# Rows scattered into an expert-ordered table, the last batch routed in halves, shorter logits, and both ends of a two-layer kernel rewritten

## The reference, cut to what matters

```python
x1 = layernorm(x + window_attention(x))        # 16 heads, rotary, window of 64
x2 = layernorm(x1 + rwkv_channel_mix(x1))      # r, k, v products, relu squared
x3 = layernorm(x2 + linear_attention(x2))      # feature map, 16 heads
# last sublayer: a whole block with its own residuals, then the last layer norm
h  = layernorm(x3, ln1); x4 = x3 + causal_attention(h) @ Wproj
z  = layernorm(x4, ln2)                        # N = 4096 rows
gates = softmax(z @ Wgate); top 2 of 8 experts
pos = cumsum(mask, axis=0) * mask - 1          # place of a token among its expert's, in token order
keep = pos < capacity                          # capacity = 1024
exp_in[e, pos] = z[token]                      # (8, 1024, 256), zeros where nothing falls
exp_out = gelu(exp_in @ W1 + b1) @ W2 + b2     # 256 -> 1024 -> 256
x5 = x4; x5[token] += gate * exp_out[e, pos]
out = layernorm(x3 + x5)                       # the sum around the sublayer
```

## Time and profile before

| | |
|---|---|
| median of 3 runs | 1914.5 us (1913.64 to 1915.02) |
| the profiled execution: its time, its span | 1915.56 us, 1913.8 us |
| busy: TensorE, its weight loads | 1713.6 us (90%), 1106.0 us |
| busy: VectorE, ScalarE, GpSimd | 1018.5, 879.8, 831.4 us |
| mean granted TensorE clock | 0.948 |
| DMA | 124.17 MB, mean 65 GB/s |

### The profile page before, as it was taken

How to read it: one execution, slowest core, us unless ns; L and a number is a source line. 1 busy time by engine, 2 the same in 40 slices (tenths; PEclk the granted TensorE clock), 3 DMA queues, 4 the chain that set the end, 5 groups by cost and what they waited for, 6 DMA issues and landing times. The chain is left out here.

```text
span 1913.8 us, 32830 instructions
## 1 busy us (share of the span) xinstructions
PE 1713.6 (90%) x10804; PEld 1106.0 (58%) x10804; DVE 1018.5 (53%) x2375; ACT 879.8 (46%) x1855; POOL 831.4 (43%) x1247
## 2 busy tenths in 40 slices
PE   4798998999999999999989999998279999999970
PEld 3565765665477666556756545545246776666750
DVE  3457676868566986847698677775101110001115
ACT  2355463657755364765536566765031222222202
POOL 4574564522377552248663243324434333234220
PEclk9899999999999899999999999999589999999995
DMA  5615235032344222254502223420313332333115
GB/s 190 92 19 67 35 79 68 14 55 68 53 74 100 24 34 35 68 68 69 112 2 40 52 50 41 68 67 22 121 59 85 83 69 49 70 85 88 23 17 181
DMA packets 93059, 124.17 MB, mean 65 GB/s; under 512 B 14065, under 2 KB 63153, under 8 KB 92737
## 3 DMA queue, kind: packets, MB, share of 16 engines
q1 hardware_dynamic: 78560, 105.24, 26.8%
q0 software_dynamic: 14336, 16.83, 5.3%
HBM read 45.70 MB, written 25.56 MB: 37 GB/s over the span
## 5 line engine op out<-in xcount | busy, mean ns | idle before, releaser
L1026 ACT ACTIVATE b_probs<-b_psum 128x512 f32<-128x512 f32 (+3 forms) x896 | 417.9, 544 | 179.3 <-PE b_psum L896 177.7
L1277 DVE TENSOR_REDUCE b_mneg<-b_psum 128x2 f32<-128x384 f32 (+5 forms) x608 | 333.5, 593 | 94.0 <-PE b_psum L883 92.4
L1372 POOL TENSOR_SCALAR_AFFINE_SELECT b_probs<-b_probs 128x512 f32<-128x512 f32 (+1 forms) x400 | 240.0, 611 | 314.8 <-ACT b_probs L1026 304.3
L883 PE MATMUL b_psum<-b_qk 96*128 96x192 bf16 (+4 forms) x1280 | 298.9, 300 | 6.0 <-DVE b_before L1249 2.7
L896 PE MATMUL b_psum<-b_qk 99*128 99x192 bf16 (+5 forms) x1344 | 262.8, 290 | 9.7 <-DMA b_qk<-b_mrow 6.4
L1656 DVE TENSOR_TENSOR b_ye<-b_psum,b_b2b 128x512 f32<-128x512 f32 x32 | 22.1, 692 | 428.9 <-PE b_psum L1611 428.9
L1635 ACT ACTIVATE b_hid<-b_psum,b_b 128x512 f32<-128x512 f32 x128 | 88.0, 687 | 317.9 <-PE b_psum L1602 317.9
L1564 POOL DMA_INDIRECT before_last_norm<-b_ye,b_ids x64 | 99.5, 1555 | 301.0 <-DMA before_last_norm<-b_ye,b_ids 156.2
L1611 PE MATMUL b_psum<-b_w,b_hid 128*128 128x256 f32 x1024 | 222.4, 379 | 0.8 <-ACT b_hid L1635 0.8
L1602 PE MATMUL b_psum<-b_xgt,b_w 128*128 128x512 f32 x512 | 221.7, 594 | 0.0
L1611 PEld LDWEIGHTS b_psum<-b_w,b_hid 128*128 128x128 f32 x1024 | 193.9, 190 | 27.6 <-ACT b_hid L1635 1.6
(11 more groups left out here) (212 smaller groups left out, 2431.6 us busy)
## 6 DMA issues: line engine op xcount, KB each, us to landing
b_qk<-b_split SPq DMA_DIRECT2D x372, 128.0 KB, 4.9
b_w<-in_W SPq DMA_DIRECT2D x16, 1024.0 KB, 7.8
b_src<-in_x SPq DMA_DIRECT2D x4, 1024.0 KB, 6.2
before_last_norm<-b_early SPq DMA_DIRECT2D x4, 1024.0 KB, 4.9
b_o<-before_last_norm SPq DMA_DIRECT2D x4, 1024.0 KB, 5.4
before_last_norm<-b_o SPq DMA_DIRECT2D x4, 1024.0 KB, 4.5
normed<-b_y SPq DMA_DIRECT2D x4, 1024.0 KB, 5.2
b_rows<-before_last_norm SPq DMA_DIRECT2D x8, 512.0 KB, 7.8
```

The costliest lines, as they stand in the source:

```text
L883: ins = pe.matmul(out[:, i, :], q[0:KS, h, P * t:P * t + P], q[0:KS, HG + h, a:e], start=not last, stop=True, skip_group_check=True)
L1026: act.activation(probs_of((g, h2, t), a, e)[:, heads[0]:heads[-1] + 1, :], bank, ACT.Exp, scale=SCALE).then_inc(s.exp_done, 1)
L1277: dve.tensor_reduce(out, in_bank(("max",) + x[1:], heads, e - a), AX.X, ALU.max, negate=True).then_inc(s.max_read, 1)
L1372: ins = pool.affine_select(out=block, in_=block, pattern=[[0, HG], [1 if ahead else -1, z - y]], compare_op=ALU.is_ge, fill=none, base=y - ...
```

## The change

- **Straight into an expert-ordered table.** `normed` and its store `z_out` are gone. A table `slot_rows` in DRAM has one row for each of the 8 x 1024 slots. SP fills it with zeros early (`zeros`, 8 DMAs of 1 MB). When a batch's slot numbers are known (`spot`, the first half of the old `place`), GpSimd scatters the z rows from `y` there, 128 rows of 1 KB per DMA, 16 DMAs per batch (`put`), beside the 16 entry scatters. `y` is free when the puts have landed. In the experts' block SP loads each expert's rows with two plain DMAs (`load_tokens`); the gathers are gone, and the entries are needed only for gates and for the way back, so they are turned in the middle of the first expert.
- **Halves.** The last batch's routing from `logits` on is done in two parts of four tiles. The first part's puts are issued before the block ends, the second part's and all entry scatters after.
- **Logits.** Four products side by side, in four groups of 32 columns: the gate weights (padded to 32 columns) are the stationary operand, half of the part's tokens move through each. ScalarE copies the result back, and one small product per tile (`choose`) with a matrix of two ones per column adds the two halves of the contraction and turns it.
- **Start.** The identity and x come first, in halves; the first projection's weights have a semaphore of their own; small constants are issued by ScalarE and waited for at the first use in layer 0.
- **End.** The last expert's hidden parts are ordered by columns (512, 256, 256) with the values of finished columns between them, and its last two tiles are passed on singly. The last norm stands in the experts' block, without a block's end before it; its table is loaded behind the last Gelu. GpSimd computes scale and shift, ScalarE applies three rows of four and VectorE one.

```diff
+        self.AHEAD = {("place", B - 1): 25.0, ("put", B - 1): 25.0}
-                  [self.known(*x, self.batch[g] - 1) for x in (("z_out",), ("z_turn", 1, 1), ("x4", 3))]))
+                  [self.known(*x, self.batch[g] - 1) for x in (("put", TOPK - 1, NT - 1), ("z_turn", 1, 1), ("x4", 3))]))
+        for e in range(E_):
+            add(("zeros", e), "SP", 0.5, ("rotate", 0, 7), ("divide", e // 4, e // 2 % 2))
...
+        parts = self.parts_of(b)
+        for r, tiles in enumerate(parts):
+            size = len(tiles) / NT
+            before = ("place", r - 1, b) if r else self.known("place", 0, b - 1)
+            add(("logits", r, b), "PE", 0.25 + 0.87 * size, ("z_take", tiles[-1] // 4, 1, b))
+            add(("logit_take", r, b), "ACT", 0.1 + 0.42 * size, ("logits", r, b))
+            add(("choose", r, b), "PE", 1.6 * size, ("logit_take", r, b))
...
+            add(("spot", r, b), "DVE", 1.1 + 0.4 * size, ("position", r, b), ("index", r, b),
+                *[self.known(kind, TOPK - 1, NT - 1, b - 1) for kind in ("put", "scatter") if not r])
+            add(("place", r, b), "DVE", 0.9 + 0.4 * size, ("spot", r, b), ("gates", r, b))
+            if b < B - 1 or r + 1 < len(parts):
+                for kind, ready in (("put", "spot"), ("scatter", "place"))[:1 if self.halved(b) else 2]:
+                    for k in range(TOPK):
+                        for t in tiles:
+                            add((kind, k, t, b), "POOL", 1.28, (ready, r, b))
...
+def put_rows(pool, u, k, t, z_slots, rows_put):
+    pool.indirect_dma_start(
+        out=z_slots, out_offset=bass.IndirectOffsetOnAxis(ap=u.write_at[:, k, t:t + 1], axis=0),
+        in_=u.y[:, t, :], in_offset=None, bounds_check=E_ * CAP - 1, oob_is_err=False).then_inc(rows_put, 16)
...
+                        for side in range(2):
                             for c in range(NC):
+                                k = NC * side + c
+                                ins = pe.matmul(out[32 * k:32 * k + 32, 0:n], u.wgate[:, c, :],
+                                                u.xtr[:, c, P * tiles[0] + n * side:P * tiles[0] + n * side + n],
+                                                start=True, stop=True, tile_position=(0, 32 * k), skip_group_check=True)
+                    elif kind == "choose":
...
+                            ins = pe.matmul(out[:, E_ * t:E_ * t + E_], u.xtr[:, 0, at:at + P], u.pairs[:, i // n, :],
+                                            start=True, stop=True)
...
+                        if b and not x[1]:
+                            dve.wait_ge(slots_gathered, 16 * TOPK * NT * b)
+                            dve.wait_ge(rows_put, 16 * TOPK * NT * b)
+                        ins = dve.tensor_tensor(u.write_at[:, :, some], place, keep, ALU.add)
...
                     if not windowed[g] and not plan.place_of(g) and b:
-                        dve.wait_ge(s.z_out, 16 * b)
+                        dve.wait_ge(rows_put, 16 * TOPK * NT * b)
...
@@ experts, SP
+            sp.wait_ge(rows_put, 16 * TOPK * NT * B)
+            load_tokens(sp, 0, u, s, z_slots)
+            load_tokens(sp, 1, u, s, z_slots)
+            load_expert(sp, 1, u, s, w1_dram, w2_dram)
             sp.wait_ge(slots_gathered, 16 * TOPK * NT * B)
             sp.dma_start(u.slot_rows[:, :, :], slots_dram.rearrange("(r p) o -> r p o", p=P)).then_inc(s.rows_in, 16)
...
+            sp.wait_ge(s.summed, 16 * E_ * CT)
+            for h in range(HALVES):
+                sp.dma_start(u.rows[:, 4 * h:4 * h + 4, :], rows(x4_dram, h)).then_inc(rows_in[h], 16)
@@ experts, GpSimd
+            for k in range(TOPK):
+                for t in LAST_TILES:
+                    put_rows(pool, u, k, t, z_slots, rows_put)
+            for k in range(TOPK):
+                for t in range(NT):
+                    scatter_entry(pool, u, k, t, slots_dram, slots_gathered)
...
+                link(pool.tensor_tensor(scales, root, root, ALU.mult))
+                link(pool.tensor_tensor(scales, scales, u.last_var[:, four], ALU.mult))
+                link(pool.tensor_scalar(scales, scales, -0.5, 1.5, ALU.mult, ALU.add))
+                link(pool.tensor_tensor(scales, scales, root, ALU.mult))
+                link(pool.tensor_tensor(u.shifts[:, four], u.last_mv[:, four, 0], scales, ALU.mult))
+                pool.tensor_scalar(u.shifts[:, four], u.shifts[:, four], -1.0, None, ALU.mult).then_inc(last.scale_ready, 1)
...
@@ experts, TensorE, last expert
+                for part, whole in enumerate((pieces_of(e)[:2], pieces_of(e)[2:3], pieces_of(e)[3:])):
+                    ahead = min(NF * (part + 1) + 2, len(parts))
+                    for k, x in parts[begun:ahead]:
+                        hidden(e, k, *x)
+                    begun = ahead
+                    pe.wait_ge(s.h_done, 16 * e + NF * (part + 1))
+                    for tiles in whole:
+                        values(e, tiles)
...
@@ set-up, ScalarE
+            act.wait_ge(cleared, 1)
+            act.dma_start(u.wgate[:, :, 0:E_], a["wgate"]).then_inc(later, 16)
+            for n in LATER_SMALL:
+                act.dma_start(made[n][:], a[n]).then_inc(later, 16)
+            for n in LATER_ROWS:
+                act.dma_start(made[n][:, :], a[n].partition_broadcast(P).rearrange("p o d -> p (o d)")).then_inc(later, 16)
             take_turned(act, u.xa[:, :, 1:T + 1], u, s, 0)
+            act.dma_start(slots_dram.rearrange("(r p) o -> r (p o)", p=P), a["empty"]).then_inc(later, 16)
+            act.dma_start(x4_dram[N:N + P, :], a["spare_rows"]).then_inc(later, 16)
```

More of the change, by code:

```diff
@@ L56 @@
 EARLY = 1
+HALVED = True
 BANK = 512
@@ L216 @@
                 "back": "keep",
-                "oc_turn": "oc_take", "oc_pj": "oc_y", "z_turn": "z_take", "logits": "top", "position": "place",
+                "oc_turn": "oc_take", "oc_pj": "oc_y", "z_turn": "z_take", "logits": "logit_take", "choose": "top", "position": "spot",
                 "o_turn": "o_take", "pj": "y1", "x1_turn": "x1_take", "r": "r_low", "k0": "relu", "v0": "gated",
@@ L447, in describe_norm, with parts_of, part_with, halved @@
                     self.add((out + "_dve", t + 2, b), "DVE", 0.35, (name + "_scale", h, b), read[1])
+    def parts_of(self, b):
+        return [range(NT)] if not self.halved(b) else [range(4), range(4, NT)]
+    def part_with(self, b, t):
+        return [t in tiles for tiles in self.parts_of(b)].index(True)
+    def halved(self, b):
+        return HALVED and b == B - 1
     def describe_route(self, b):
         add = self.add
-        add(("x3_in", b), "SP", 3.0, ("x3_out", b), self.known("out1", 3, b + 1), self.known("x4_out", b - 1),
-            self.known("z_out", b - 1))
+        add(("x3_in", b), "SP", 3.0, ("x3_out", b), self.known("out1", 3, b + 1), self.known("x4_out", b - 1))
         for h in range(2):
@@ L841, in _ @@
                     b = plan.batch[2 * g]
+                    if t == 0 and not g:
+                        pe.wait_ge(first_weights, 32)
                     if t == 0 and not first:
@@ L1097, in _ @@
                             dve.wait_ge(s.src_in, 16 * b)
+                        if not b and not x[1]:
+                            dve.wait_ge(later, LATER_COUNT)
+                            dve.tensor_scalar(u.bk[:, :], u.bk[:, :], 1.0, None, ALU.add)
+                            chained(dve.tensor_scalar(u.bq_plus[:, :], u.bq[:, :], 1.0, None, ALU.add))
                         ins = sum_and_stats(b, x, "pj", u.src, u.src, u.norms[0])
@@ L1198, in _ @@
                     elif kind == "top":
-                        done(dve, b, "logits")
-                        chained(dve.tensor_copy(u.lg[:, :, :].rearrange("p t e -> p (t e)"), bank_of("logits", b)[:, 0:NT * E_]))
-                        for t in range(NT):
+                        some, n = part_of(b, x[1]), len(plan.parts_of(b)[x[1]])
+                        done(dve, b, "choose", x[1])
+                        chained(dve.tensor_copy(u.lg[:, some, :], routed_bank("choose", x[1], b)[:, some, :]))
@@ L1719, in statistics @@
+            link = dve_chain(dve, last.dve_chain)
+            def apply(h):
+                dve.wait_ge(last.scale_ready, h + 1)
+                i = 4 * h + 3
+                dve.tensor_scalar(u.rows[:, i, :], u.rows[:, i, :], u.last_mv[:, i, 0:1], u.scales[:, i:i + 1],
+                                  ALU.subtract, ALU.mult).then_inc(last.dve_ready, 1)
+            for h in range(HALVES):
                 dve.wait_ge(rows_in[h], 16)
@@ L1866, in _ @@
             dve.memset(u.ones16[:, :], 1.0)
-            dve.wait_ge(loaded, 16 * (count + 3))
+            dve.memset(u.wgate[:, :, :], 0.0).then_inc(cleared, 1)
+            dve.wait_ge(rows_in[0], 32)
+            for i in range(2):
+                dve.tensor_tensor(u.pairs[:, i, :], u.id32[:, 64 * i:64 * i + E_], u.id32[:, 64 * i + 32:64 * i + 32 + E_], ALU.add)
+            dve.wait_ge(loaded, 16 * count)
             for i, t in enumerate(bf16_tables):
```

485 lines of the change are left out of this document (245 added, 240 removed).

## The result

The kernel after takes 1867.04 us (median of 4 runs, 1865.49 to 1870.92) against 1914.07 (1913.3 to 1915.02) in the same comparison: ratio 0.9753, 95% interval 0.9739 to 0.9768. The forecast was 1871.0 with 0.95 on faster. The profiled execution is the fastest of its four (1865.49 us, span 1863.7, clock 0.959); the spans differ by 50.1, the medians by 47.0.

What follows compares the result with a forecast made beforehand. TensorE bounds attention and experts; about 170 us around them are serial. Terms -10.5 + 4 - 19.9 + 0.5 - 13.3 - 4.3 = -43.5 take 1915.56 to 1872.1, 1871.0 for the median; range 1857 to 1888.

Steps and rivals of the forecast that it cites:

- Set-up: Before the first projection: reordered loads, with ScalarE issuing 13 DMAs at 0.48 us, start it at 14.4; gain 10.5 us.
- Attention: Attention stage: logits gain 3 us, puts cost 6, zero fills 1; sum +4 us (-3 to +20).
- the 6 charged: Attention stage: cost of GpSimd's added puts, 2 us for each of three batches (0 to 15).
- until the second half's z is turned nothing changes: Last batch: its path stays as before up to that turn, at 1342.4 us; no cost put there.
- The 1.6 us per put: GpSimd's puts: price if VectorE's two-port operations keep it from writing descriptors; time some 5 us later.
- The hold of `y`: Attention, batch 3: y comes free near 1297 us, and waiting outputs cover the 32 us; 0 charged, 5 at the other end.
- The rival of a re-planned order: Attention stage: queues planned anew with truer scatter costs cut TensorE's idle time by 8 us, to 1863; chance 0.10.
- Last batch: From the last z to the experts: half routing and direct puts start TensorE at 1378.5 instead of 1398.35; gain 19.9 us.
- Behind the last product: After the last expert: earlier scatter-adds and no block's end (3.3) before the norm; gain 13.3 us (10 to 14).
- The stall that I say is included: Last expert: 1 us of extra TensorE stall, said to be included in the 13.3 us gain.
- Last norm: Final norm: work shared with GpSimd and ScalarE gives a period of 2.45 us per half batch; gain 4.3 us (0 to 6).
- The lock that the earlier trace let one fear: Last norm: VectorE and GpSimd exclude each other on SBUF; 0.2 or so a half, 2 us in all.

Runs made afterwards that it cites:

- e10: Kernel after with the attention block closed without GpSimd's drain, repeated with more rounds; 1863.05 us, ratio 0.9731 to the kernel before.
- e2: Kernel after with the last batch routed whole instead of in halves, drain kept; 1870.99 us, ratio 0.9777 to the kernel before.
- e3: Kernel after with the last batch routed whole and the attention block closed without GpSimd's drain; 1874.3 us, ratio 0.9804 to the kernel before.
- e12: Kernel before with both blocks closed without GpSimd's drain; 1908.89 us against 1914.45, ratio 0.9971.
- e6: Kernel after with the last norm's scale chain back on VectorE and rows shared two and two; 1874.54 us, ratio 0.9798 to the kernel before.
- the control: Kernel after, unchanged, timed again beside later runs; 1869.48 us, ratio 0.9760 to the kernel before.
- e8: Kernel after with each put of batches 0 to 2 issued twice, the second into a spare table; 1871.96 us, ratio 0.9786 to the kernel before.
- e11: Kernel after without the 48 row puts of batches 0 to 2, so the experts see zeros there; 1862.75 us, ratio 0.9728 to the kernel before.
- e4: Kernel after with ScalarE's thirteen early DMAs and all later weight loads issued by SP at attention's start; 1869.05 us, ratio 0.9765 to the kernel before.

## Why the prediction was right, step by step

The total was met with some luck. The attention stage cost 5 to 7 us more than its term, and the last batch won 4 and the norm 2.5 more than theirs.

- *Set-up* (-10.5, came -10.9): the mechanism was ScalarE's issues. They cost 0.56, not SP's 0.48 by which I had priced them. The takes then started at 11.5 instead of my sum's 10.4, and the first product at 14.0, within 0.4 of the sum.
- *Attention* (+4, came +6.0 to the last turn of z in the pair of profiles, some +9 to +11 by the medians): the puts took 1.28 as assumed, 1.00 busy and 0.30 between, and cost likely 5 or 6 of the 6 charged. The logits won 0.7 per batch, 2.2 in all, instead of 3. The step that was wrong is "until the second half's z is turned nothing changes": the first half's route stood ahead of it and cost 3.2, a term put at nothing. That leaves some 3 to 5 us open; the route of batch 2 that moved ahead and the zero fills weren't tried alone.
- *The software DMAs.* The Trainium skill (SBUF — State Buffer, the box on the trap of software DMA) says that a VectorE operation in a two-port mode keeps GpSimd from writing descriptors. The 1.6 us per put that the prediction took for it had no row behind it. The 56 puts in this stage were busy 1.00 us on average and 1.27 at most, the undisturbed 0.97, so little of the kind shows.
- *The hold of `y`* (0, and no wait for it shows): the reason given was wrong. I kept batch 2's route where before had it and let two waiting outputs fill 32 us. The order was planned anew with the puts as a predecessor of the output, and the route moved ahead instead. What that cost the work it displaced is part of the open 3 to 5. The rival of a re-planned order had the right mechanism and a gain of 8 that didn't come.
- *Last batch* (-19.9, came -23.9 from the last turn of z): three errors met. I had the first half's puts start 10.4 us after the turn of z (1350.0 - 1339.65) and let the second half's wait for them. They started with the turn, so the second half's could have started 8.8 sooner than I had them against that turn, as e10's do (12.8 behind it, not 21.6). Against this I took 1.0 for the block's end, from a trace in which the drain was over before anyone waited. With puts under way until just before, it held GpSimd 6.7 us longer. The landing was 2.45, not 4.0, and the load 0.3 quicker: 8.8 - 6.7 + 1.6 + 0.3 = 4.0. Halves were worth 8.0 on the path, as e2 shows, and 14.8 without the drain (e3 against e10: 42.98 - 28.13), less the 3.2 ahead of it.
- *Behind the last product* (-13.3, came -14.1): the last scatter starts 10.0 nearer to TensorE's end (13.4 to 3.4), and the loads follow it 4.1 sooner (7.9 to 3.8), 3.8 of it the drain (e12), where I had 3.3. The stall that I say is included isn't in my sum (9.9 + 3.3 = 13.2), and none came.
- *Last norm* (-4.3, came -6.8): the mechanism right, the size low. Six operations of GpSimd took 1.65 us where I had summed 2.0, and the period was 2.28, not 2.45: 7 x 0.17 = 1.2. I had also taken 4.3 where the sum said 4.7; some 0.9 lies in the norm's ends. e6 gives 6.4 back. The lock that the earlier trace rows let one fear isn't seen: GpSimd's small operations stayed at 0.19 to 0.24 beside the statistics. And the VectorE operation of the earlier trace rows has one input, so its 2.20 shows a wait beside GpSimd's adds, and bears out no rule on operations with two inputs.

In the pair of profiles -43.5 became -50.1: attention 2.0 less, against 4.0 more of the last batch, 2.5 of the norm, 0.9 of the experts, 0.8 of the end and 0.4 of the set-up. In medians the distance is 4.0, and 1.5 in the control's.

## What to carry over

In this kernel closing a block held GpSimd in a drain behind its own transfers, though nobody needed them yet. In a profile look for the DRAIN of GpSimd's queue at each block's end and for what stands behind it. Its price was zero in the old trace, where another engine ended later, and came out when the change made that engine faster. Cut the stages at an event that the change leaves in place, or a cost and a gain hide each other. And where a planner writes the order, a new condition moves work rather than adding a wait: price it by what must now come earlier, and check how far apart two executions of one program lie before reading a few us in two traces.

## What the runs showed of the hardware

- GpSimd's drain ended 8.6 us behind the end of its last 1 KB-row put in after, some 4.6 in e8 and e11, and 4.0 behind the last 8-byte scatter in before. SP's load, which waits on a semaphore for the second half's puts to land, starts 2.45 behind the last one's start. Behind the last 8-byte scatter in before it was 4.0; why is open.
- A scatter of 128 rows took GpSimd the same 1.28 us for 8 bytes and for 1 KB a row (after).
- A DMA issued by ScalarE took 0.45 to 0.70 us of its queue. The same thirteen took 0.43 to 0.66 issued by SP in e4.
- One program's attention stage differed by 6 us between executions, 0.3% of the kernel.
